# A graph network on one core: edges packed without holes into 806 tiles, register-held places, and a sort that signals once per 14 columns

## The reference, cut to what matters

```python
for l in range(3):                                   # first part
    X = einsum('ne,ref->rnf', out, weights[l])       # 9 transformed copies of every node
    msg = X[edge_type, src] + biases[l][edge_type]   # one row of 128 floats for each edge
    hidden = segment_sum(msg, dest, num_segments=N)  # sums by the node that the edge ends on
    out = relu(hidden) if l + 1 < 3 else hidden
x = layernorm(x + out)
# second part: softmax over each node's edges of beta * cosine(x[row], x[col]), weighted sum of x[col]
x = layernorm(x + attention)
```

## Time and profile before

| what | us |
|---|---|
| median of three runs | 4264.41 |
| the profiled execution | 4270.03 |
| its span, first to last instruction | 4268.3 |
| up to the first scatter of the sort | 114.6 |
| scatters and sort, until the first gather | 439.4 |
| layer 0: first gather to the start of the next X | 1081.5 |
| X of layer 1, until the first gather | 55.7 |
| layer 1 | 1078.5 |
| X of layer 2 | 54.6 |
| layer 2, to the first transposition | 1068.7 |
| second part | 375.3 |

### The profile page before, as it was taken

One profiled execution on the slowest core, in us unless ns is written; L12 is line 12 of the kernel. 1 busy time (PEld: TensorE's weight loads), 2 busy tenths in 40 slices (PEclk: granted clock), 3 DMA queues, 4 the chain that ended last, 5 costly groups with the idle time before them and its releaser, 6 DMA issues.

```text
span 4268.3 us, 55641 instructions
## 1 busy us (share of the span) xinstructions
PE 3096.6 (73%) x13925; PEld 1821.7 (43%) x13926; DVE 2434.5 (57%) x9103; ACT 857.6 (20%) x1992; POOL 2752.9 (64%) x2839
## 2 busy tenths in 40 slices
PE   7799957676776678667667667777775655656998
PEld 4455424333433334333334333344333434434776
DVE  9888855554555556555554554465554333335999
ACT  2599801001001000001001001001000000002665
POOL 0777777777777772777777777647777777772000
PEclk9899979999899997999998998898997555556999
DMA  4100013333433437333333333553433222224564
GB/s 157 42 2 2 2 45 83 78 71 80 80 72 78 81 72 175 70 72 76 83 72 74 84 74 71 71 175 76 83 72 85 53 53 53 53 53 76 185 192 141
DMA packets 377130, 343.02 MB, mean 80 GB/s; under 512 B 263666, under 2 KB 327722, under 8 KB 376712
## 3 DMA queue, kind: packets, MB, share of 16 engines
q0 software_dynamic: 90368, 165.49, 19.7%
q1 hardware_dynamic: 83112, 113.25, 8.0%
q10 hardware_dynamic: 203360, 60.73, 5.9%
HBM read 232.12 MB, written 107.13 MB: 79 GB/s over the span
## 4 chain that ended last, share of the span: by engine, by line
POOL 63%; issue 21%; PE 9%; DVE 5%; DMA 2%; ACT 1%; SPq 0%; POOLq 0%; DVEq 0%; ACTq 0%
POOL region L817 55%; POOL scattered_edges L800 8%; PE ps L958 2%; PE ps L929 2%; PE ps L986 2%; DMA region<-x_of_type,arrays 1%; DVE region L340 1%; DVE region L608 1%; PE ps L961 1%; PE ps L919 1%; DVE region L580 0%; PE ps L908 0%; DVE arrays L368 0%; DVE arrays L379 0%; DVE region L599 0%
## 5 line engine op out<-in xcount | busy, mean ns | idle before, releaser
L817 POOL DMA_INDIRECT region<-x_of_type,arrays x2520 | 2415.7, 959 | 918.9 <-issue 764.9
L908 PE MATMUL ps<-oh,region 128*128 128x102 f32 x5040 | 1261.3, 340 | 725.9 <-DMA region<-x_of_type,arrays 707.0
L441 DVE TENSOR_SCALAR oh<-iota_w,arrays 128x102 f32<-128x102 f32 x2528 | 724.3, 290 | 1703.7 <-PE ps L908 1701.4
L919 PE MATMUL ps<-region 128*128 128x510 f16 x4200 | 1402.0, 410 | 346.8 <-issue 195.8
L908 PEld LDWEIGHTS ps<-oh,region 128*128 128x128 f32 x5040 | 1000.1, 228 | 1454.9 <-DMA region<-x_of_type,arrays 1281.2
L919 PEld LDWEIGHTS ps<-region 128*128 128x128 f16 x4200 | 434.5, 113 | 549.8 <-issue 527.2
L505 DVE TENSOR_TENSOR region<-region,ps 128x102 f32 x2520 | 646.1, 256 | 3.6 <-issue 3.2
L1048 ACT COPY region<-ps 128x510 f32<-128x510 f32 x155 | 89.8, 579 | 2482.8 <-PE ps L919 2482.3
L800 POOL DMA_INDIRECT scattered_edges<-region x304 | 332.8, 1095 | 207.0 <-DVE ends L398 109.3
L887 PE MATMUL ps<-region 128*128 128x420 f16 x2016 | 362.6, 342 | 24.9 <-ACT region L1025 24.9
L1025 ACT ACTIVATE region<-region 128x128 f16<-128x128 f16 x1008 | 348.8, 394 | 39.7 <-DVE region L418 29.6
(11 more groups left out here) (173 smaller groups left out, 1486.4 us busy)
## 6 DMA issues: line engine op xcount, KB each, us to landing
region<-x_of_type,arrays POOLq DMA_INDIRECT x2520, 2.6
edge_counts<-region ACTq DMA_DIRECT2D x155, 255.0 KB
arrays<-edge_counts SPq DMA_DIRECT2D x40, 960.0 KB, 5.0
x_of_type<-region SPq DMA_DIRECT2D x50, 576.0 KB, 3.9
edge_absent<-region ACTq DMA_DIRECT2D x155, 127.5 KB
region<-edge_absent SPq DMA_DIRECT2D x40, 480.0 KB, 4.4
x_of_type<-x0st SPq DMA_DIRECT2D x51, 192.0 KB, 1.8
scattered_edges<-region POOLq DMA_INDIRECT x304
```

The source lines that it names most:

```text
L441: ins = nc_.tensor_scalar(oh[:, t % U, 0:RB], iota_r, rowf[:, t % NT:t % NT + 1], None, ALU.is_equal)
L817: pool.indirect_dma_start(out=grow[:, t % GR, :], out_offset=None, in_=xt, in_offset=bass.IndirectOffsetOnAxis(ap=gix[:, t:t + 1], axis=0) ...
L908: mm = pe.matmul(ps[:, 6 + n % 2, t * RB:(t + 1) * RB], grow[:, u % GR, :], oh[:, u % U, 0:RB], start=True, stop=True)
L919: mm = pe.matmul(ps[:, c, 0:CW], cl[:, q % CR, c * P:(c + 1) * P], cr[:, q % CR, :], start=False, stop=False, skip_group_check=True)
```

## The change

The edges are now laid without holes: group after group, into GT = 806 tiles, of which the last alone is partly empty. A tile in which a group ends and the next begins is fetched once and used twice. PE and DVE still work through NT = 840 uses in each layer. For a use the program computes the number of its tile (the use's number less the number of tiles that were used twice so far), and keeps two lists in SBUF: the place of that tile (tile modulo GR = 62, times 128) and, for every four uses, the tile that must have landed. PE loads them into registers.

- **POOL** issues 806 gathers in a layer into 62 places; before a group of four from tile t on it waits for use t - 29.
- **SP** waits for the 62 gather semaphores one after the other and adds 1 to a single one (`s_seq`), on which PE waits against a register once for every four uses.
- **PE** takes the one-hot (102 columns) as the weights and the tile (128 columns) as the moving operand, so a block is now 102 nodes by 128 features. Of the cells, five columns share one register load, and each column has one register wait, for the fourth of the five banks, where there were three.
- **DVE** adds blocks of 102 partitions by 128 to `hn`. Since `hn` has the nodes on partitions, PE turns its 31 blocks behind every layer (`turn_sums`), and DVE moves them to `hB` in eight pieces, with relu between layers. Behind the third layer the 25 blocks are turned as before, out of `hB`.
- **Sort:** 28 buffers for the one-hots, and one signal of PE, and one wait of DVE and ACT, for every 14 columns. DVE computes the two lists in 20 steps that stand between the columns of the sort, one every 16 columns from column 68 on.
- **Behind the sort** the row of X of each tile has to be found by tile and not by use: DVE isolates the lower part of the words, PE turns it (7 transpositions), ACT copies it, PE multiplies it with selecting matrices `pick` (8 pieces of 32 to 160 columns, 998 together, float32), and DVE takes the result as `gix`. Only then may POOL begin.

The diff, cut to its core:

```diff
-GR = 24
+GR = 62
 BODY = 24
+PAIRS = 8
-KR = 4
+KR = 28
+KS = 14
...
+    GT = -(-E // P)
+    LAP = MB - 1
...
             for t in range(EP):
                 k = t % KR
                 q, c = (cols[:, 4 * t + n:4 * t + n + 1] for n in range(2))
-                if t >= KR:
-                    dve.wait_ge(s_put, t - KR + 1)
+                if t >= KR and t % KS == 0:
+                    dve.wait_ge(s_put, (t - KR) // KS + 1)
                 nc_.tensor_scalar(hot_q[:, k, :], iota_s[:, 0:P], q, None, ALU.is_equal).then_inc(s_hot, 1)
                 nc_.tensor_scalar(oh_s[:, k, :], iota_s, c, None, ALU.is_equal).then_inc(s_cell, 1)
+                if t % 8 == 4 and t // 8 in MIDWAY:
+                    plan(MIDWAY.index(t // 8))
...
+            step(nc_.tensor_tensor(w, wide[:, 0:NT], w, ALU.add))
+            step(nc_.tensor_scalar(v, w, (1 << ROW_BIT) - 1, None, ALU.bitwise_and))
+            step(nc_.tensor_copy(wide[:, 0:NT], v), "words")
+
+            step(nc_.tensor_scalar(g, w, -1.0, None, ALU.add))
             step(nc_.tensor_scalar(v, g, ROW_BIT, None, ALU.arith_shift_right))
-            nc_.tensor_copy(rowf[:, 0:NT], v)
+            step(nc_.tensor_copy(rowf[:, 0:NT], v))
+            dve.wait_ge(s_pt, 1)
+            nc_.tensor_scalar(gix[:, 0:512], ps[:, 4, 0:512], -1.0, 0.0, ALU.add, ALU.max)
+            step(nc_.tensor_scalar(gix[:, 512:GT], ps[:, 5, 0:GT - 512], -1.0, 0.0, ALU.add, ALU.max), "rows")
...
-                    h = hA[:, bass.ds(bs[t], RB)]
-                    nc_.tensor_tensor(h, h, ps[:, 6 + n % 2, t * RB:(t + 1) * RB], ALU.add).then_inc(s_add, 1)
+                    h = hn[0:RB, bass.ds(bs[t], D)]
+                    nc_.tensor_tensor(h, h, ps[0:RB, 6 + n % 2, t * D:(t + 1) * D], ALU.add).then_inc(s_add, 1)
...
+            def pass_on(l):
+                for t in range(GT):
+                    sp.wait_ge(s_g[t % GR], 16 * (ROUNDS * l + t // GR + 1))
+                    sp.sem_inc(s_seq, 1)
...
-                for t in range(NT):
-                    n = NT * l + t
-                    if t % SLOTS == 0 and n >= GR:
-                        pool.wait_ge(s_used, n // SLOTS - RINGS + 1)
+                for t in range(GT):
+                    last = t + SLOTS - 1 - GR + LAP
+                    if t % SLOTS == 0 and t + SLOTS - 1 >= GR:
+                        pool.wait_ge(s_used, NT // SLOTS * l + last // SLOTS + 1)
...
-                    pe.wait_ge(s_g[u % GR], i * (16 * BODY // GR) + 16 * ((first + u) // GR + 1))
+                    if u % PAIRS == 0:
+                        at = slots_at((i * BODY + u) // PAIRS)
+                        due = values_of(pe, tile_due, (i * BODY + u) // PAIRS, GT, PAIRS // SLOTS, 1)
                     if t == 0:
+                        reg_wait(pe, s_seq, due[u % PAIRS // SLOTS] + GT * l)
                         pe.wait_ge(s_oh, i * (BODY // SLOTS) + (first // SLOTS + n + 1))
                         pe.wait_ge(s_add, i * BODY + (first + u + SLOTS))
-                    mm = pe.matmul(ps[:, 6 + n % 2, t * RB:(t + 1) * RB], grow[:, u % GR, :], oh[:, u % U, 0:RB],
+                    mm = pe.matmul(ps[0:RB, 6 + n % 2, t * D:(t + 1) * D], oh[:, u % U, 0:RB], grow[:, bass.ds(at[u % PAIRS], D)],
                                    start=True, stop=True)
...
-                            ready = values_of(pe, b7, k, CG * (MB - 1) + 1, 1)[0]
+                            if q % CR == 0:
+                                ready = values_of(pe, b7, k // CR, CG * (MB - 1) + 1, CR)
                             pe.wait_ge(s_co, k + 1)
-                        if c % 2 == 0:
-                            reg_wait(pe, s_cz, ready + min(c + 1, CG - 1))
+                            reg_wait(pe, s_cz, ready[q % CR] + (CG - 1))
...
+            def turn_sums(l):
+                pe.wait_ge(s_add, NT * l + 2 * SLOTS)
+                for n in range(HN):
+                    if n >= XB:
+                        pe.wait_ge(s_feat, HN * (l - 1) + n - XB + 1)
+                    for t in range(min(SLOTS, MB - SLOTS * n)):
+                        b = SLOTS * n + t
+                        mm = pe.transpose(ps[:, 5 + n % XB, t * RB:(t + 1) * RB], hn[0:RB, b * D:(b + 1) * D],
+                                          ident[0:RB, 0:RB])
+                    mm.then_inc(s_tn, 1)
+                pe.wait_ge(s_feat, HN * l)
```

More of the change, by code:

```diff
@@ L61, in gnn_program @@
     TURNS = NT // BODY
-    KW = NT + GR
-    RINGS = GR // SLOTS
+    KW = NT + BODY
+    GT = -(-E // P)
+    LAP = MB - 1
+    ROUNDS = GT // GR
+    assert GT + LAP <= NT and ROUNDS * GR == GT and GR >= LAP + BODY and NT % PAIRS == 0 and PAIRS % SLOTS == 0
+    SLOT_SHIFT = 16
+    SLOT_MUL = -(-(1 << SLOT_SHIFT) // GR)
+    assert GT * SLOT_MUL < 1 << 24 and all(t * SLOT_MUL >> SLOT_SHIFT == t // GR for t in range(GT))
+    HN = -(-MB // SLOTS)
+    TC = -(-NT // P)
+    PW = P + 32
+    SLO = [max(0, P * c - 32) for c in range(TC)]
+    SHI = [min(GT, P * c + P) for c in range(TC)]
+    assert LAP <= 32
     CP = 304
@@ L200, in gnn_program @@
         unit = part(NP).rearrange("p (b d) -> p b d", b=NB)
-        used[0] = max(GR * D, NP) + NP
+        hA = part(NP)
         ring = part(RING * SC).rearrange("p (u w) -> p u w", u=RING)
@@ L413, in _ @@
+            MIDWAY = range(8, 8 + 2 * (13 + TC), 2)
             for t in range(EP):
@@ L529, in _ @@
                         take_tiles(l, i, False)
+            for n in range(HN):
+                take_turned(L, n, False)
             def moments(z, b):
@@ L1027, in _ @@
                 ins.then_inc(s_scaled, 1)
+            for n in range(2):
+                act.wait_ge(s_wt, n + 1)
+                m = min(512, NT // P * P - 512 * n)
+                ins = act.copy(wordt[:, 512 * n:512 * n + m], ps[:, 6 + n, 0:m])
+                if 512 * n + m < NT and n:
+                    ins = act.copy(wordt[0:NT % P, NT - NT % P:TC * P], ps[0:NT % P, 6 + n, m:m + P])
+                ins.then_inc(s_wc, 1)
             act.wait_ge(s_d, marks["ends"])
```

192 lines of the change are left out of this document (143 added, 49 removed).

## The result

The changed kernel takes 4210.52 us, the median of four runs (4200.54 to 4214.52), against 4264.88 for the kernel before in the same comparison: a ratio of 0.9868 (0.9851 to 0.9886), 54 us less. The forecast was 120 us less, 4145, and its range ended at 4190. The direction was right, the size less than half of it. The profiled execution took 4214.52 us, 55.5 less than that of before, with a span of 4212.8.

A forecast was written before the change was run, and what follows sets the result against it. POOL's issue of gathers was taken to set the pace. Terms -127.5 - 14 + 20 + 6 - 5 + 0.6 gave -120 us, from 4264.4 to 4145 us; range 4110 to 4190.

The forecast's parts named there:

- The gathers: POOL's gathers in all three layers: 102 fewer at 1.25 us each, -127.5 us (bound -129).
- the 163 us of slack: PE's waits for landings in layer 0, taken to absorb PE's other work and DVE's longer add, priced at 0.
- Ends of the layers and turning: Layer ends without hole tiles, -14 us (0 to -25); 31 PE transpositions behind each layer, +20 us (14 to 26).
- The way to the first gather: Stretch from the sort's table to POOL's first gather: 10.5 us instead of 4.6, +6 us (3 to 12).
- The sort: Scatters beside the sort, before layer 0: lock on two columns breaks, average wait slightly shorter, -5 us (-17 to +25).
- The sort lets the scatters go: Rival: scatters fall to 1.27 us, the sort's end becomes the bound, -17 instead of -5, total 4122; 15%.
- PE as the pace with cells: Rival: over 0.14 us more per PE use keeps 84 cell turns' length; gathers save 25.5, total 4247; 6%.
- Starving scatters: Rival: POOL gets in only where DVE stops, 2.36 + 0.30 us per scatter, +308 us, total 4457; 5%.
- the packing's -14: Layer ends: no tiles of holes requesting one row, so last landings come sooner, -14 us (0 to -25).

## Why the prediction was wrong, step by step

**The gathers, the step that failed.** The number is right (102 fewer, all on the path), and so is the price where DVE is quiet. The sentence that failed is: "The contention with DVE that makes 1.268 out of 1.25 belongs to the cells, whose number does not change, so I price a gather at 1.25". It holds the contention fixed because its other party, the cells' one-hots, is fixed. But how much of it POOL bears depends on the add that stands between them (1005 ns for 962 in the kernel before, with nothing else changed), and the change has cut that add to 102 partitions. Measured, 1.32, 1.31 and 1.27 us per gather, 94 us over three layers; -127.5 became -34.8. The one place in the prediction that speaks of that add, "DVE's add grows by 0.03 us", has its duration right (256 to 282 ns) and its effect wrong: it looked only at time, and put all of PE's and DVE's changes into the 163 us of slack of the earlier trace rows. Slack of PE is no cover for what an operation of DVE does to POOL.

With full partitions this term is -46.6, -45.2 and -45.1 us, -137 in all: 34 gathers at 1.26 to 1.27 and a pitch shorter by 0.003 to 0.004. Then the time is even below the forecast's 4145, at 4113. In the changed kernel luck covered some 20 us of this miss: the sort, below, gave more than was forecast.

**Ends of the layers and turning, +6 together, measured -2.6.** The parts came out near. Two timelines of the changed kernel, at the end of layers 0 and 2:

```profile
1598.91 0.94 POOL L925 DMA_INDIRECT region<-x_of_type,arrays  x1 [0.30 <-issue]
...
1611.37 4.64 PE L1069 MATMUL ps<-ident,region 102*128 102x102 f32 x31 [2.06 <-DVE region L596]
1616.57 5.62 PE L1080 MATMUL ps<-wsb,hB 128*128 128x384 f32 x12 [0.57 <-DVE hB L602]
...
3823.14 0.95 POOL L925 DMA_INDIRECT region<-x_of_type,arrays  x1 [0.30 <-issue]
3831.92 5.50 PE L1069 MATMUL ps<-ident,region 102*128 102x102 f32 x31 [2.06 <-DVE region L596]
...
3837.99 4.72 PE L988 MATMUL ps<-ident,hB 128*128 128x128 f32 x25 [0.57 <-DVE hB L604]
```

To the first transposition it takes 12.5 us in layer 0 (forecast: about 12) and 8.8 in layer 2 (11); turning with the copy behind it takes 5.2 and 6.1 (7). That is 0.4 and 0.7 us more than the 17.2 and 14.2 of before (and 0.1 more at the end of layer 1), so holes saved and turning spent nearly the same. Turning was priced at 6.3 us for 31 transpositions and took 4.64 and 5.50. The rest of the -2.6 is X, which no term had: from PE's first product to the next layer's first gather it takes 54.3 and 52.7 us for 55.7 and 54.6, at a granted clock of 0.97 and 1.00 for 0.93 and 0.95; the second part is 0.5 us shorter.

**The way to the first gather, +6, measured +4.9.** The changed kernel's timeline:

```profile
524.18 1.10 DVE L516 COPY arrays<-ps 128x420 f32<-128x420 f32 x2 [7.80 <-PE ps L1002]
...
526.44 1.03 DVE L537 TENSOR_TENSOR arrays<-arrays 128x840 int32<-128x840 f32 x1
...
530.59 3.92 PE L1023 MATMUL ps<-region 128*128 128x128 f32 x16
...
535.94 0.99 POOL L925 DMA_INDIRECT region<-x_of_type,arrays  x1 [25.92 <-DVE arrays L546]
```

9.5 us from the add to the first gather (forecast 10.5), against 4.6 in the earlier trace rows. The selecting products take 3.92 us, near the 3.6 that were taken for half the rate, not the 1.8 of the full one; the granted clock was 0.54 in them, the lower of the two levels for nearly all of it.

**The sort, -5, measured -25.** The first line above carries the answer: DVE waits 7.80 us for PE's last matmuls and not for the table, so the sort sets the end. In the list of rivals this was "The sort lets the scatters go", with 15%, and its scatters of 1.27 us came true. Even its -17 was short: in the kernel with this part alone the first gather came 24.6 us earlier (554.04 to 529.47), the 20.7 us of DVE's wait and 3.9 by which the sort itself ended sooner (DVE's copies begin at 522.57 for 526.47). In the changed kernel the add comes 23.0 us earlier, at 526.44 for 549.41. The prediction cited the Trainium skill, "SBUF — State Buffer", section "SBUF: two separate sides", by which denser DVE work would only keep POOL from its descriptors. For columns in a steady stream the runs show the reverse: 1122 ns with a gap after each column, 964 and 977 without one. (One scatter did wait for a whole run of DVE, 2.36 us beside four casts.) As the prediction read, the old pitch of 1.43 us was exactly two columns; that a lock on DVE's short gaps made it is only argued. Shown is that the pitch ends with the signal per 14 columns and the 28 buffers; which of the two did it, or the buffers' new place in that run, was not taken apart.

**The other rivals.** PE as the pace with cells (4247): the layers did keep their old length nearly, as that rival foretold, but for another reason; POOL waits for PE 19.8 us in all. In all they gave 34.8 us, near its 25.5. A test by the layers' lengths alone would have taken it for true; what ended POOL's idle time told it apart. Starving scatters (4457) did not come.

**What stays open.** How an add on 96 or 102 partitions keeps POOL longer from its work beside f16 operations of DVE that both kernels have. Shown is only the exchange: POOL's gathers 955 to 964 ns in the mean and the cells' second one-hot 366 to 375, or gathers 1005 to 1014 and the one-hot 348 to 353. The Trainium skill, in "SBUF — State Buffer", section "Who interferes with whom", says that a VectorE instruction with at most one SBUF input, outside the two-port modes, does not contend with GpSimd. The add has one input in SBUF and one in PSUM; alone by that rule its partitions could not matter, and here they move 96 us.

## What to carry to other kernels

When a change cuts an operation down to the part of the partitions that it needs, look at the neighbours on the other engines and not only at the operation: in this kernel the 26 idle partitions cost 96 us, and adding zeros on them cost DVE nothing (281 ns for 282). Other operations and other kernels were not tried. Contention between two engines is not a constant of their pair that can be carried over by counting: price it anew if any instruction of either changes shape, and put both ends into the range. And where padding asks for a row of memory, let each partition ask for another one; in the kernel before it gave 22 us, by one operand and a table of 128 numbers. That is a gain at the same place as the packing's -14, so it is not to be added to the packing's without a run.

## What the runs showed of the hardware that was not expected

- Beside the cells' f16 one-hots, gathers of POOL take 955 to 964 ns in the mean when DVE's adds (one input in PSUM) are on 128 partitions, and 1005 to 1014 when they are on 96 or 102, in both kernels; the add's columns (102 or 128) and its duration (256 or 281 ns) make no difference. The difference lies in a tail: no gather over 1.13 us against 75 to 86 over 1.2 in 900 us. Without the cells it is 944 to 946 ns either way.
- DVE operations in f16, 14 columns without a pause, do not lengthen POOL's scatters: 964 ns, where they took 1122 beside columns with a short gap. DVE's one-hot of 840 columns is lengthened instead, 433 to 532 ns.
- Gathers of 128 requests for one row of HBM land only every 1.69 us, gathers of 128 requests for different rows as fast as POOL issues them, every 1.25.
- The kernel before, 4265 to 4273 us on the other chips, took 5147 on one, where the traces have waits for a remote releaser that the others' lack.
